# The end of a factorisation-machine kernel in three blocks of 256, 160 and 96 columns instead of two of 320 and 192

## The reference

```python
x_reg = input_data @ W_lin.T + b_lin
emb = input_data @ factors                                   # 1024 x 16
sum_squared = jnp.square(emb.sum(axis=1))
squared_sum = (jnp.square(input_data) @ jnp.square(factors)).sum(axis=1)
h = jax.nn.relu(emb @ W1.T + b1)                             # 128 wide
h = jax.nn.relu(h @ W2.T + b2)                               # 64 wide
dnn_out = h @ W3.T + b3
x = x_reg + 0.5 * (sum_squared - squared_sum)[:, None] + dnn_out
x = 0.5 + jax.nn.sigmoid(x) * 5.0
```

## Time and profile before

| | |
|---|---|
| median of 3 runs | 136.48 us (136.44 to 136.8) |
| the profiled execution | 136.62 us |
| its span, first to last instruction | 134.3 us |
| TensorE busy | 106.3 us (79%) |
| ScalarE busy | 65.1 us (48%) |
| VectorE busy | 53.4 us (40%) |
| read from HBM | 52.16 MB, 388 GB/s over the span |
| last matmul of the pieces' squares to the last scaling | 130.91 to 132.43 us |

### The profile page before, as it was taken

The page is one execution under the profiler, slowest core; times in us unless marked ns, Lnnn a source line. Parts: engine busy times, 40 slices in busy tenths (PEclk is TensorE's granted clock), DMA queues, the critical chain, the costliest instruction groups (busy, mean ns, idle before and its releaser), DMA issues.

```text
span 134.3 us, 2688 instructions
## 1 busy us (share of the span) xinstructions
PE 106.3 (79%) x1034; PEld 29.9 (22%) x1034; DVE 53.4 (40%) x52; ACT 65.1 (48%) x74; POOL 11.6 (9%) x49
## 2 busy tenths in 40 slices
PE   6089976965976966967978969977977889889991
PEld 1022211111211111111112312211211123336760
DVE  0391550450550451352351393152253155555840
ACT  4030752661752652562573496372473374447741
POOL 5026011011011011011011001111000000000000
PEclk9999999999999999999999999999999999999999
DMA  4999999999999999999999999999999999999500
GB/s 120 394 366 439 420 439 415 434 410 439 420 439 420 439 420 439 420 434 424 429 429 420 439 420 434 420 429 424 429 429 429 418 412 427 428 403 411 193 5 1
DMA packets 4580, 52.25 MB, mean 389 GB/s; under 512 B 518, under 2 KB 650, under 8 KB 1502
## 3 DMA queue, kind: packets, MB, share of 16 engines
q1 hardware_dynamic: 4574, 52.16, 92.8%
HBM read 52.16 MB, written 0.00 MB: 388 GB/s over the span
## 4 chain that ended last, share of the span: by engine, by line
DMA 62%; PE 29%; SPq 2%; issue 2%; DVE 2%; ACT 1%; DVEq 0%; ACTq 0%
DMA xr<-in_x_groups 53%; PE p_lin L427 22%; DMA xr<-in_x_end 10%; PE p_tot L427 2%; PE p_sq L427 2%; PE p_h L508 2%; DVE sq L362 1%; SPq L212 1%; PE p_h L532 1%; ACT sg L302 1%; SPq L210 0%; SPq L209 0%; SPq L208 0%; ACT lin L288 0%; ACT qs L338 0%
## 5 line engine op out<-in xcount | busy, mean ns | idle before, releaser
L275 ACT ACTIVATE sq<-xr 128x1536 f32<-128x1536 f32 (+1 forms) x40 | 48.5, 1263 | 47.5 <-DMA xr<-in_x_groups 47.4
L362 DVE TENSOR_TENSOR sq<-xr 128x1536 f32<-128x1536 f32 x20 | 35.1, 1758 | 56.9 <-DMA xr<-in_x_groups 56.9
L427 PE MATMUL p_lin<-xr,wr 128*17 128x512 f32 x320 | 38.3, 594 | 16.2 <-DMA xr<-in_x_groups 16.2
L427 PE MATMUL p_lin<-sq,wz 128*18 128x512 f32 x320 | 38.4, 595 | 2.7 <-DVE sq L362 1.2
L427 PEld LDWEIGHTS p_lin<-xr,wr 128*17 128x17 f32 x320 | 8.1, 97 | 45.3 <-POOL wr L250 24.7
L427 PEld LDWEIGHTS p_lin<-sq,wz 128*18 128x18 f32 x320 | 8.3, 97 | 32.3 <-ACT sq L275 19.5
L283 ACT ACTIVATE sq<-xr 128x384 f32<-128x384 f32 (+1 forms) x17 | 9.6, 617 | 6.7 <-DMA xr<-in_x_end 6.7
L250 POOL COPY wr<-hd x20 | 5.9, 296 | 73.8 <-PE p_lin L427 73.3
L369 DVE TENSOR_TENSOR sq<-xr 128x640 f32<-128x640 f32 (+1 forms) x15 | 9.8, 695 | 6.2 <-DMA xr<-in_x_end 6.2
L427 PE MATMUL p_lin<-xr,hd 128*17 128x320 f32 (+1 forms) x128 | 8.9, 381 | 0.9 <-DMA xr<-in_x_end 0.9
L427 PE MATMUL p_lin<-xf,hd 128*17 128x512 f32 x4 | 3.6, 1049 | 3.7 <-DMA xf<-in_x_first 3.7
(11 more groups left out here) (49 smaller groups left out, 36.6 us busy)
## 6 DMA issues: line engine op xcount, KB each, us to landing
xr<-in_x_groups SPq DMA_DIRECT2D x20, 2048.0 KB, 15.4
xr<-in_x_end SPq DMA_DIRECT2D x4, 1280.0 KB, 13.4
xr<-in_x_end SPq DMA_DIRECT2D x3, 768.0 KB, 13.6
hd<-in_head SPq DMA_DIRECT2D x1, 934.0 KB, 4.7
xr<-in_x_end SPq DMA_DIRECT2D x1, 576.0 KB, 14.5
xf<-in_x_first SPq DMA_DIRECT2D x1, 512.0 KB, 5.9
xl<-in_x_rest SPq DMA_DIRECT2D x1, 336.0 KB
xr<-in_x_end SPq DMA_DIRECT2D x1, 192.0 KB, 14.5
```

Source lines behind the costliest of these rows:

```text
L275: nc.scalar.activation(sq[:, s, c:c + n, :], xr[:, s, c:c + n, :], ACT.Square).then_inc(act_squared, 1)
L362: nc.vector.tensor_tensor(sq[:, s, 0:BY_DVE, :], xr[:, s, 0:BY_DVE, :], xr[:, s, 0:BY_DVE, :], ALU.mult).then_inc(dve_squared, 1)
L427: return nc.tensor.matmul(out, lhsT, rhs, start=False, stop=False, skip_group_check=True)
```

## The change

Columns 512 to 1023 end in three blocks, of 256, 160 and 96 columns, instead of two of 320 and 192, and in 13 pieces instead of nine. Only the last block's squares go to `p_sq`; block 2 collects its squares with its products in `p_lin[0]`, and block 3 takes `p_lin[1]`, which is cleared after `rest` has been copied (now for both blocks). A block's total lies in quarters, on partitions 0, 32, 64 and 96, a quarter of the block long, so that sigmoid, square and scaling work on 128 partitions and half as many columns as before. The embedding sum is written first on the place of the total, squared by ScalarE, and then overwritten by the linear term (`start=True`), so `linear(k)` waits for `gsq_ready[k]`. One more store. The lists of all engines for the end are written anew. The memset of `gsq` and the wait for it go.

```diff
-BLOCKS = ((0, 512), (512, 320), (832, 192))
-PIECES = ((1, 0, (2, 2), (2, 2)), (1, 8, (2, 2), (2, 2)), (1, 16, (2, 2), (2, 2)), (1, 24, (2, 2), (2, 2)),
-          (2, 0, (2, 2), (2, 2)), (2, 8, (2, 2), (2, 2)), (2, 16, (2, 2), (2, 2)), (2, 24, (2, 2), (2,)),
-          (2, 30, (2,), ()))
+BLOCKS = ((0, 512), (512, 256), (768, 160), (928, 96))
+LAST = len(BLOCKS) - 1
+PIECES = ((1, 0, (4,), (4,)), (1, 8, (4,), (4,)), (1, 16, (4,), (4,)), (1, 24, (4,), (4,)),
+          (2, 0, (4,), (4,)), (2, 8, (4,), (4,)), (2, 16, (4,), (4,)), (2, 24, (4,), (4,)),
+          (3, 0, (2, 2), (2, 2)), (3, 8, (2, 2), (2, 2)), (3, 16, (2, 2), (2, 2)), (3, 24, (2, 1), (2, 1)),
+          (3, 30, (1,), (1,)))
...
+        def quarter(k, q):
+            c, n = BLOCKS[k]
+            return slice(c + q * n // 4, c + (q + 1) * n // 4)
+        def line(k):
+            c, n = BLOCKS[k]
+            return slice(c // 4, (c + n) // 4)
+        def end_bank(k):
+            return p_lin[k % 2]
...
-            for k in range(3):
+            for k in range(len(BLOCKS)):
                 sp.wait_ge(y_ready[k], 1)
-                sp.dma_start(out[cols(k)].rearrange("(u b) -> u b", u=2), y[64:P:32, row(k)]).then_inc(y_stored, 16)
-            sp.wait_ge(y_stored, 48)
+                sp.dma_start(out[cols(k)].rearrange("(q b) -> q b", q=4), y[0:P:32, line(k)]).then_inc(y_stored, 16)
+            sp.wait_ge(y_stored, 16 * len(BLOCKS))
...
-            nc.gpsimd.memset(gsq[:, :], 0.0).then_inc(pads_set, 1)
...
             def embedding_square(k):
                 act.wait_ge(p_es_done[k], 1)
-                nc.scalar.activation(gsq[0:64, row(k)], tot_bank(k)[0:64, row(k)], ACT.Square).then_inc(gsq_ready[k], 1)
+                nc.scalar.activation(gsq[:, line(k)], tot_bank(k)[:, line(k)], ACT.Square).then_inc(gsq_ready[k], 1)
...
# ScalarE's end
-            for i in range(4):
+            for i in range(5):
                 square_end(i)
-            square_end(4)
             act.wait_ge(p_lin_done[1], 1)
             copy_lin(1, 0)
             copy_lin(1, 1)
-            layer1(1)
             nc.scalar.copy(rest[:, :], p_lin[1][:, BLOCKS[1][1]:HALF]).then_inc(rest_copied, 1)
             square_end(5)
+            layer1(1)
             embedding_square(1)
             square_end(6)
             square_end(7)
-            square_end(8)
+            square_end(8, 0)
+            square_end(8, 1)
+            square_end(9, 0)
+            square_end(9, 1)
+            square_end(10, 0)
+            embedding_square(2)
+            square_end(10, 1)
+            square_end(11, 0)
             sigmoid(1)
-            embedding_square(2)
+            square_end(11, 1)
+            square_end(12, 0)
+            embedding_square(3)
+            sigmoid(2)
             act.wait_ge(squares_done, 1)
-            nc.scalar.copy(qs[:, :], p_sq[:, 0:BLOCKS[2][1]]).then_inc(qs_ready, 1)
-            sigmoid(2)
+            nc.scalar.copy(qs[:, :], p_sq[:, 0:BLOCKS[LAST][1]]).then_inc(qs_ready, 1)
+            sigmoid(3)
...
# VectorE's end
-            for i in range(5):
+            for i in range(6):
                 square_end(i)
             dve.wait_ge(p_h1_done[1], 2)
             layer1(1, p_h1[1], BLOCKS[1][1] // 2)
-            square_end(5)
+            square_end(6)
             layer2(1)
-            square_end(6)
             square_end(7)
+            square_end(8, 0)
+            square_end(8, 1)
             dve.wait_ge(rest_copied, 1)
             copy_block(2)
+            square_end(9, 0)
+            square_end(9, 1)
             dve.wait_ge(p_h1_done[2], 1)
             layer1(2, p_h1[0], BLOCKS[2][1])
+            square_end(10, 0)
+            square_end(10, 1)
+            square_end(11, 0)
+            square_end(11, 1)
+            copy_block(3)
+            layer2(2)
+            square_end(12, 0)
+            dve.wait_ge(p_h1_done[3], 1)
+            layer1(3, p_h1[1], BLOCKS[3][1])
             scale(1)
-            layer2(2)
             scale(2)
+            layer2(3)
+            scale(3)
...
# TensorE: terms of the total
-            def terms(k):
-                for u in range(2):
-                    mm = add_mm(tot_bank(k)[32 * u:32 * u + 1, row(k)], pr[:, C_SE:C_SE + 1], lin[:, part(k, u)])
+            def embedding_sum(k):
+                for q in range(4):
+                    mm = nc.tensor.matmul(tot_bank(k)[32 * q:32 * q + 1, line(k)], pr[:, C_SE:C_SE + 1],
+                                          lin[:, quarter(k, q)], start=True, stop=False, skip_group_check=True)
                 mm.then_inc(p_es_done[k], 1)
-                for u in range(2):
-                    add_mm(tot_bank(k)[64 + 32 * u:65 + 32 * u, row(k)], pr[:, C_SX:C_SX + 1], lin[:, part(k, u)])
+            def linear(k):
+                pe.wait_ge(gsq_ready[k], 1)
+                for q in range(4):
+                    nc.tensor.matmul(tot_bank(k)[32 * q:32 * q + 1, line(k)], pr[:, C_SX:C_SX + 1],
+                                     lin[:, quarter(k, q)], start=True, stop=False, skip_group_check=True)
...
# TensorE's end, the new list
+            multiply_end(4)
+            layer1(1)
+            multiply_end(5)
+            embedding_sum(1)
+            add_squares_end(4)
+            add_squares_end(5)
+            multiply_end(6)
+            pe.wait_ge(rest_copied, 1)
+            clear(p_lin[1][:, 0:BLOCKS[3][1]])
+            pe.wait_ge(h1a_ready[1], 1)
+            pe.wait_ge(h1b_ready[1], 1)
+            layer2(1)
+            linear(1)
+            add_squares_end(6)
+            multiply_end(7)
+            add_squares_end(7).then_inc(p_lin_done[2], 1)
+            multiply_end(8)
+            multiply_end(9)
+            pe.wait_ge(lin_ready[2], 1)
+            first_layer(p_h1[0], BLOCKS[2][1], lin[:, cols(2)]).then_inc(p_h1_done[2], 1)
+            pe.wait_ge(sg_ready[0], 1)
+            embedding_sum(2)
+            embedding_square(1)
+            layer3(1)
+            add_squares_end(8)
+            multiply_end(10)
+            add_squares_end(9)
+            multiply_end(11)
+            multiply_end(12).then_inc(p_lin_done[3], 1)
+            pe.wait_ge(h1b_ready[2], 1)
+            layer2(2)
+            linear(2)
+            embedding_square(2)
+            add_squares_end(10)
+            pe.wait_ge(lin_ready[3], 1)
+            first_layer(p_h1[1], BLOCKS[3][1], lin[:, cols(3)]).then_inc(p_h1_done[3], 1)
+            pe.wait_ge(sg_ready[1], 1)
+            embedding_sum(3)
+            layer3(2)
+            add_squares_end(11)
+            add_squares_end(12).then_inc(squares_done, 1)
+            pe.wait_ge(h1b_ready[3], 1)
+            layer2(3)
+            linear(3)
+            embedding_square(3)
+            pe.wait_ge(qs_ready, 1)
+            n = BLOCKS[3][1] // 4
+            for q in range(4):
+                add_mm(tot_bank(3)[32 * q:32 * q + 1, line(3)], pr[:, C_SX:C_SX + 1], qs[:, q * n:(q + 1) * n])
+            layer3(3)
```

More of the change, by code:

```diff
@@ L63 @@
 C_HALF = C_SX + 1
-C_ALL = C_HALF + 2
+C_ALL = C_HALF + 4
 HD_P = ALL * LIN
@@ L99, in fm_kernel @@
         lin = sb("lin", [P, B])
-        rest = sb("rest", [P, BLOCKS[2][1]])
-        qs = sb("qs", [P, BLOCKS[2][1]])
+        rest = sb("rest", [P, BLOCKS[2][1] + BLOCKS[3][1]])
+        qs = sb("qs", [P, BLOCKS[LAST][1]])
         h1 = sb("h1", [P, B])
         h2 = sb("h2", [P, HALF])
-        gsq = sb("gsq", [P, HALF])
-        sg = sb("sg", [P, HALF])
-        y = sb("y", [P, HALF])
+        gsq = sb("gsq", [P, B // 4])
+        sg = sb("sg", [P, B // 4])
+        y = sb("y", [P, B // 4])
         warm = sb("warm", [P, 1])
@@ L277, in squares, with square_end @@
                     c += n
[L279 to L285, removed]
+            def square_end(i, j=0):
+                c = PIECES[i][1] + sum(PIECES[i][2][:j])
+                n = PIECES[i][2][j]
+                if j == 0:
+                    act.wait_ge(end_landed[i], 16)
+                nc.scalar.activation(piece(sq_end, i, c, n), piece(xe, i, c, n),
+                                     ACT.Square).then_inc(act_end_squared, 1)
             def copy_lin(k, u):
@@ L297, in embedding_square @@
                 act.wait_ge(p_es_done[k], 1)
-                nc.scalar.activation(gsq[0:64, row(k)], tot_bank(k)[0:64, row(k)], ACT.Square).then_inc(gsq_ready[k], 1)
+                nc.scalar.activation(gsq[:, line(k)], tot_bank(k)[:, line(k)], ACT.Square).then_inc(gsq_ready[k], 1)
             def sigmoid(k):
                 act.wait_ge(p_tot_done[k], 1)
-                nc.scalar.activation(sg[64:P, row(k)], tot_bank(k)[64:P, row(k)], ACT.Sigmoid,
-                                     bias=bias[64:P, :]).then_inc(sg_ready[k], 1)
+                nc.scalar.activation(sg[:, line(k)], tot_bank(k)[:, line(k)], ACT.Sigmoid,
+                                     bias=bias[:, :]).then_inc(sg_ready[k], 1)
             with act.Fori(0, ROUNDS[0]) as r:
@@ L363, in squares, with square_end @@
```

(39 more changed lines are left out.)

18 lines of the change are left out of this document (1 added, 17 removed).

## The result

The changed kernel takes 137.81 us (median of 8 runs, 137.35 to 138.65) against 136.52 for the kernel before (8 runs, 136.42 to 136.8): a ratio of 1.0088, 95% interval 1.0076 to 1.0101. It is 0.9% slower, where the prediction said 135.4 and faster. The profiled execution took 137.89 us with a span of 136.0.

The account below looks back on a forecast made before the run. The input stream bounds the kernel to its end, then a mostly TensorE tail. Tail 3.34 us for 4.77, stream 0.30 longer: 136.62 - 1.13 = 135.49, less 0.14 to the median: 135.35, said 135.4, range 134.8 to 136.2.

Parts of the forecast that it names:

- TensorE then waits for piece 9 at 125.98: it has caught up, and goes on without a stop: TensorE's queue near the stream's end: idle until piece 9 lands at 125.98, then multiplies 11 and 12 done by 128.27.
- four rivals: Narrow work doesn't shrink (0.12), a new wait (0.13), a longer stream (0.06), the change not doing what it says.
- A new wait takes the gain: In the tail, ACT's operations cost 0.08 us more each, so `qs` comes 1.0 us late: 136.4, no change; chance 0.13.
- The slower side: Input stream lengthened 0.6 to 2.5 us by block 1's 8,192-byte rows, at the far end 137.8; chance 0.06, half slower.
- The sign: Whole kernel's outcome against the kernel before: faster 0.81, same 0.14, slower 0.05.
- three signs of being wrong: Block 1's pieces spaced above 2.6 us, ACT reaching `qs` after 130.3, or TensorE never waiting after 122.
- The third, the spacing of the pieces: In the input stream: the forecast is wrong if block 1's pieces are more than 2.6 us apart; 2.49 expected.
- The stream: Input transfers: same bytes in 13 transfers for 9, 0.30 us longer, last landing at 127.96 instead of 127.66.
- the durations of the narrow operations: ACT and DVE work in the tail, scaled to fewer columns: sigmoid 0.28, relu 0.27, scaling 0.17, copies 0.26 and 0.24 us.
- A term of the total: On TensorE, four quarter matmuls of 24 or 40 columns, eight instructions: 0.12 us, bounds 0.05 and 0.20.
- the lower of my bounds: Price of a term of the total by column count alone: 0.05 us, against 0.20 as the upper bound.
- The tail without the stops: From last landing to last scaling: 3.34 us for 4.77, last scaling ending at 131.30 instead of 132.43.

Follow-up runs that it names:

- e4: Kernel before the change, each matmul of block 2's pieces (192 columns) cut in two of 96, 256 instructions more for the same columns: 139.2 us (1.0184).
- e1: Changed kernel with 32 one-column padding matmuls (64 TensorE instructions) put ahead of the pieces: 137.5 us, 1.0064 to the kernel before.
- e3: Changed kernel with 96 one-column padding matmuls (192 instructions) put ahead of the pieces: 140.57 us, 1.0292 to the kernel before.
- e9: Changed kernel with the last block's products and squares joined in one matmul per chunk, 128 TensorE instructions fewer: 136.86 us, 1.001 to the kernel before.
- e12: The joined kernel (e9) with 48 one-column padding matmuls: 137.11 us (1.0053); the two runs between had 16 and 32: 137.09 and 136.84 us.
- e2: Changed kernel with 64 one-column padding matmuls (128 instructions) put ahead of the pieces: 138.11 us, 1.0107 to the kernel before.
- e7: Kernel before the change with 32 one-column padding matmuls (64 instructions) ahead of the pieces, as control: 136.53 us (0.9994).

## Why the prediction was wrong

- **The step that failed** is "TensorE then waits for piece 9 at 125.98: it has caught up, and goes on without a stop". The queue was priced by columns and by the spacing of eight instructions, and nothing in the sum was for bringing the instructions in. In the trace TensorE reached squares 6 at 124.14 (0.5 later than the 123.6 of the forecast) and stopped, never waited for piece 9, and stopped twice more, 2.55 us in all. e4 shows that the number of instructions alone costs 2.6 us in a kernel without the change, e1 to e3 that the stops belong to every 256th instruction and not to the work.
- None of the four rivals was this one. "A new wait takes the gain" came nearest, but it named ScalarE's squares and ended at 136.4, no change. The slower side was given to the stream, whose pieces came exactly on time; that its far end, 137.8, is the time that was measured is chance. The sign thus got 0.05.
- Two of the three signs of being wrong came true: TensorE never waited for data after 122 until the last layers, and ScalarE reached `qs` only at 131.53. The third, the spacing of the pieces, did not (2.49 us).
- **What was visible before.** The pieces' share of instructions could be counted from the diff: 32 chunks, two matmuls, four instructions each, 256 more for a third block, 66 more for its clear, layers and terms, and 104 more for the quarters in the end, with 32 in the middle: 458 more than the 2,068 of before. The page of before names instruction packets on q8 in its part 3; I read past them.
- **The stream** was right (last landing 128.05 for 127.96), and so were the durations of the narrow operations: last sigmoid 0.29, scaling 0.18, relu 0.28 and the copy of block 3 0.26, for 0.28, 0.17, 0.27 and 0.26.
- **A term of the total** was overpriced: eight instructions took 0.11 us at 64 columns and 0.07 at 40 (lines 562 and 569 in the chains), and 0.05 at 24 (e3, at 133.67), not 0.12. That goes by the columns, the lower of my bounds. The page of the Trainium skill that I weighed against it (TensorEngine Tiling (Array Packing), "Instruction Overhead") would have 40 columns cost what 60 do; here they did not.
- **The tail without the stops** would have ended at 134.04 - 2.55 = 131.49, beside 131.30 forecast. That is arithmetic, and a lower bound, since other waits may take a stop's place. No run took all the stops out of the changed kernel. e9 to e12 come nearest in the number of stops, but their tail is another, so how much of the 2.55 would come back is open.
- Open too: why the next block is asked for so late, with only 34 to 78 weight loads left.

## What to carry to other kernels

Count the instructions of a straight stretch of TensorE's list as well as its columns: 256 of them took at least 3.45 us from stop to stop in these ends, 13.5 ns each. An estimate from this: a float32 matmul, four instructions, then takes 54 ns, and eight of them took 0.33 us at 96 columns and 0.66 at 192 (41 and 82 ns each), so below about 128 columns a long stretch is bound by its code and not by its columns. A mean over the stretch is not enough, though: small layers just ahead of a boundary make a stop among matmuls of 160 columns too, as the first one here. Splitting blocks to shorten a tail multiplies instructions; wider matmuls, or one over two operands, bring them down, but joining can put other work in line behind them. An "issue" on the chain with a packet on the instruction queue some 2.4 us ahead of its end, and 256 instructions to the next one, is the sign.

## What the runs showed of the hardware

The fetch of the next block started late: with 34 to 78 weight loads left in the current one, in the three stops of the changed kernel, and 2.4 to 2.5 us ahead of the first use. In the other runs the packet starts 2.3 to 2.9 us ahead of the restart (114.26 to 116.59 in e3, 128.72 to 131.62 in e2). Padding that does nothing can make a stop where there was none (192 instructions in e3, 2.06 us), while 64 of them made none of their own in e1 and in e7. In the changed kernel the granted clock was at 0.72 of full in the mean between 34 and 40 us (3.4 us of it at 1.2 GHz, the rest at 2.4), and in e1 at full there, although TensorE had waited 2.48 us for a group in the one and 2.45 in the other; the tails, at full clock in both, stop alike.
